# Three expert mixtures: every expert over all rows, or the chosen experts over gathered rows

## The reference

```python
# level 0, inside a block that has an attention z = x + attn(...) ahead of it
logits = h @ router_w                                   # h = layernorm(x)
expert_idx = jnp.argmax(logits, axis=-1)
for e in range(E):                                      # E = 4
    gv = h @ expert_wv[e]
    gate_raw, value = jnp.split(gv, 2, axis=-1)
    y = gate_raw * jax.nn.sigmoid(gate_raw) * value @ expert_proj[e]
    out = out + jnp.where((expert_idx == e)[..., None], y, 0.0)

# level 1
router_logits = jnp.einsum('bth,eh->bte', x, router_w)  # 8 experts
topk_values, topk_indices = jax.lax.top_k(router_logits, 2)
topk_weights = jax.nn.softmax(topk_values, axis=-1)
h1 = jax.nn.gelu(jnp.einsum('bth,efh->btef', x, w1) + b1, approximate=False)
expert_outputs = jnp.einsum('btef,ehf->bteh', h1, w2) + b2
topk_expert_outputs = jnp.take_along_axis(expert_outputs, topk_indices[..., None], axis=2)
mixed_output = jnp.sum(topk_expert_outputs * topk_weights[..., None], axis=2)

# level 2
scores = jax.nn.sigmoid(x_flat @ gate_w.T + gate_bias)
top_scores, top_idx = jax.lax.top_k(scores, 2)
top_scores = top_scores / (top_scores.sum(-1, keepdims=True) + 1e-06)
...                                                     # 8 gelu experts, as in level 1
shared = (jax.nn.gelu(x_flat @ sWu.T + sbu, approximate=False) @ sWd.T + sbd) * 0.1
return (combined + shared).reshape(b, s, h)
```

## Time and profile before

| | before |
|---|---|
| median of 3 runs | 2305.26 us (2302.99 to 2305.48) |
| span of the profiled execution | 2303.5 us |
| PE busy, matrix products | 1967.1 us (85%) |
| DVE busy | 1073.2 us (47%) |
| ACT busy | 821.1 us (36%) |
| POOL busy | 338.4 us (15%) |
| moved by the main DMA queue | 58.04 MB, 9.8% of 16 engines' span |

### The profile page before, as it was taken

How to read it: one execution, slowest core, us unless ns; L and a number is a source line. 1 busy time by engine, 2 the same in 40 slices (tenths; PEclk the granted TensorE clock), 3 DMA queues, 4 the chain that set the end, 5 groups by cost and what they waited for, 6 DMA issues and landing times. The chain is left out here.

```text
span 2303.5 us, 42189 instructions
## 1 busy us (share of the span) xinstructions
PE 1967.1 (85%) x17139; PEld 1357.5 (59%) x17156; DVE 1073.2 (47%) x2487; ACT 821.1 (36%) x1451; POOL 338.4 (15%) x572
## 2 busy tenths in 40 slices
PE   6869469799899986899997868999977786776998
PEld 4637136466676664677774546777755355454776
DVE  5456545433455555631117756211133845755432
ACT  1236124322222224644331046433333142134664
POOL 2242332100000003200000042000010511411000
PEclk9759589899999996999999969999987996988999
DMA  1052311000000015100000051000000000000000
GB/s 60 1 109 55 78 42 30 29 14 15 20 22 22 22 27 109 47 10 19 19 10 6 18 114 40 10 19 19 19 33 3 0 1 3 0 15 1 5 5 10
DMA packets 44754, 62.31 MB, mean 27 GB/s; under 512 B 4529, under 2 KB 38065, under 8 KB 44337
## 3 DMA queue, kind: packets, MB, share of 16 engines
q1 hardware_dynamic: 42834, 58.04, 9.8%
q10 hardware_dynamic: 1728, 1.57, 0.3%
HBM read 25.00 MB, written 1.05 MB: 11 GB/s over the span
## 5 line engine op out<-in xcount | busy, mean ns | idle before, releaser
L1913 ACT ACTIVATE l2f_a<-l2f_bank,l2f_expert 128x512 f32<-128x512 f32 x144 | 98.7, 687 | 137.6 <-PE l2f_bank L1849 137.6
L1860 PEld LDWEIGHTS l2f_bank<-l2f_expert,l2f_a 128*128 128x128 f32 x1152 | 134.1, 192 | 16.7 <-issue 16.7
L1860 PE MATMUL l2f_bank<-l2f_expert,l2f_a 128*128 128x128 f32 x1152 | 134.3, 275 | 0.0
L2038 DVE SCALAR_TENSOR_TENSOR X<-l2f_bank,l2f_W,X 128x128 f32<-128x128 f32 x144 | 40.5, 344 | 200.2 <-PE l2f_bank L1860 200.2
L1849 PE MATMUL l2f_bank<-l2f_xT,l2f_expert 128*128 128x512 f32 x288 | 132.2, 602 | 0.0
L1913 ACT ACTIVATE l1f_a<-l1f_bank,l1f_expert 128x512 f32<-128x512 f32 x128 | 87.8, 687 | 120.1 <-PE l1f_bank L1849 120.1
L1860 PEld LDWEIGHTS l1f_bank<-l1f_expert,l1f_a 128*128 128x128 f32 x1024 | 119.2, 192 | 14.8 <-issue 14.6
L2038 DVE SCALAR_TENSOR_TENSOR X<-l1f_bank,l1f_W,X 128x128 f32<-128x128 f32 x128 | 36.0, 344 | 181.0 <-PE l1f_bank L1860 180.9
L1860 PE MATMUL l1f_bank<-l1f_expert,l1f_a 128*128 128x128 f32 x1024 | 119.3, 275 | 0.0
L1849 PE MATMUL l1f_bank<-l1f_xT,l1f_expert 128*128 128x512 f32 x256 | 117.2, 601 | 0.0
L1467 DVE TENSOR_TENSOR l1a_kv<-l1a_bank,l1a_layer 128x512 f32<-128x512 f32 x96 | 61.8, 686 | 88.0 <-PE l1a_bank L1397 88.0
(11 more groups left out here) (605 smaller groups left out, 4158.4 us busy)
## 6 DMA issues: line engine op xcount, KB each, us to landing
l2f_expert<-in_experts_l2f SPq DMA_DIRECT2D x9, 514.0 KB, 3.7
l1a_layer<-in_layers_l1a SPq DMA_DIRECT2D x12, 385.0 KB, 3.0
l1f_expert<-in_experts_l1f SPq DMA_DIRECT2D x8, 514.0 KB, 3.7
l0x_k_stack<-l0x_k_parts SPq DMA_DIRECT2D x24, 128.0 KB, 3.2
l0g_k_stack<-l0g_k_parts SPq DMA_DIRECT2D x24, 128.0 KB, 2.5
l0f_expert<-in_experts_l0f SPq DMA_DIRECT2D x4, 768.0 KB, 4.3
l1x_k_stack<-l1x_k_parts SPq DMA_DIRECT2D x24, 128.0 KB, 3.0
l2x_k_stack<-l2x_k_parts SPq DMA_DIRECT2D x24, 128.0 KB, 3.5
```

The lines of the kernel that those rows point to most:

```text
L1860: ins = pe.matmul(self.banks[4 + par][:, i * D:(i + 1) * D], self.a[:, par, c, i * T:(i + 1) * T], w2[:, c, :], start=(c == 0), stop=(c == ...
L1913: act.activation(self.a[:, par, c, :], self.banks[c][:, :], ACT.Gelu, bias=self.buf[e % 2][:, 2 * FF + c:2 * FF + c + 1]).then_inc(q["gate ...
L2038: ins = dve.scalar_tensor_tensor(out=x, in0=self.banks[4 + u % 2][:, i * D:(i + 1) * D], scalar=self.W[:, g * GI + i, e:e + 1], in1=x, op0 ...
```

## The change

`Moe` computes for each row only the experts chosen for it. In place of the loop over units it has a loop over NT tiles of 128 rows that all belong to one expert; NT is the largest number that any routing can need: 19 in l0f, 39 in l1f and l2f, and all NT are always run.

Ranking: `choose` makes the one-hot mask, `count_rows` counts on PE the rows of each expert, `place_rows` turns counts and ranks into a position for each (row, choice), `mark` and `invert` build the inverse list by one-hot products (32 pairs of DVE instructions, 16 in l0f), and `find_rows` leaves `from_row` and `to_row`, one column of 128 indices per tile. Unused places get an index out of bounds, which the DMA skips.

Tile loop: SP stores the normalised rows to DRAM (`rows`). POOL gathers a tile's rows into one of ROWS_AHEAD = 4 buffers `xg`, PE turns it (`turn`), DVE copies it (`take_x`), then `up`, `activate`, in l0f `gate`, and `down` on 128 columns; DVE copies the result (`take_y`) to one of 4 buffers `y`, and POOL scatters it to DRAM (`results`). SP reads the number of the tile's expert from memory and loads it into one of EXPERTS_AHEAD = 4 buffers. After the last scatter SP reads `results` back in four pieces, and `combine` on DVE adds both choices to X with their weights. The bias stays a product with the turned W, now after the loop. l2f's shared expert stays dense (`wide_up`, `wide_activate`, `wide_down`, `wide_add`), placed around the ranking. The packed weights of the three stages take in the constant tables that the ranking needs (l0f 3 to 254 KB, l1f 68 to 392 KB).

```diff
+SORTED = {kind: (NB * T * TOP[kind] + ROUTES[kind] * (T - 1)) // T for kind in TOP}
+ROWS_AHEAD = 4
+EXPERTS_AHEAD = 4
...
+    def turn(self, pe, j):
+        q = self.q
+        pe.wait_ge(self.gathered[j % ROWS_AHEAD], self.moved(j))
+        if j >= 2:
+            pe.wait_ge(q["xt_ready"], j - 1)
+        pe.transpose(self.banks[6 + j % 2][:, 0:T], self.xg[j % ROWS_AHEAD][:, :], self.k.ident[:, :]).then_inc(q["turned"], 1)
...
+    def down(self, pe, j):
...
+        pe.wait_ge(q["gated"], j + 1)
+        if j >= 2:
+            pe.wait_ge(q["taken"], j - 1)
...
+        for c in range(FC):
+            ins = pe.matmul(self.banks[4 + j % 2][:, 0:D], self.a[:, j % 2, c, :], w2[:, c, :], start=(c == 0), stop=(c == FC - 1))
+        ins.then_inc(q["downed"], 1)
...
     def tensor(self, pe):
...
-        for u in range(1, self.steps):
-            self.up(pe, u)
-            self.down(pe, u - 1)
...
+        pe.wait_ge(self.q["to_ready"], 1)
+        self.turn(pe, 0)
+        self.turn(pe, 1)
+        for j in range(self.NT):
+            self.up(pe, j)
+            if j + 2 < self.NT:
+                self.turn(pe, j + 2)
+            if j:
+                self.down(pe, j - 1)
+        self.down(pe, self.NT - 1)
+        if not self.gated:
+            for g in range(NG):
+                self.turn_weights(pe, g)
+                self.bias(pe, g)
...
+    def mark(self, dve, c):
...
+        for m in range(c * CHUNK, (c + 1) * CHUNK):
+            dve.tensor_scalar(self.oneP[:, m, :], w["column"], self.split[:, 0, m:m + 1], None, ALU.is_equal)
+            ins = dve.scalar_tensor_tensor(out=self.oneJ[:, m, :, :], in0=w["starts"][:, 0:NT].unsqueeze(1).to_broadcast([P, 2, NT]),
+                                           scalar=self.split[:, 1, m:m + 1], in1=codes[:, m, :].unsqueeze(2).to_broadcast([P, 2, NT]),
+                                           op0=ALU.is_equal, op1=ALU.mult)
...
     def vector(self, dve):
...
+        for j in range(self.NT):
+            if self.gated:
+                self.gate(dve, j)
+            if j + 2 < self.NT:
+                self.take_x(dve, j + 2)
+            if j:
+                self.take_y(dve, j - 1)
...
+    def gather(self, pool, j):
+        rows = (self.from_row if self.K == 2 else self.to_row)[:, j:j + 1]
+        if j >= ROWS_AHEAD:
+            pool.wait_ge(self.q["turned"], j - ROWS_AHEAD + 1)
+        pool.indirect_dma_start(self.xg[j % ROWS_AHEAD][:, :], None, self.rows[:, :], bass.IndirectOffsetOnAxis(rows, 0),
+                                bounds_check=NB * T - 1, oob_is_err=False).then_inc(self.gathered[j % ROWS_AHEAD], 16)
+
+    def scatter(self, pool, j):
+        pool.wait_ge(self.q["taken"], j + 1)
+        pool.indirect_dma_start(self.results[:, :], bass.IndirectOffsetOnAxis(self.to_row[:, j:j + 1], 0), self.y[j % ROWS_AHEAD][:, :], None,
+                                bounds_check=self.M * T - 1, oob_is_err=False).then_inc(self.scattered[j % ROWS_AHEAD], 16)
+
+    def pool(self, pool):
...
+        for j in range(ROWS_AHEAD):
+            self.gather(pool, j)
+        for j in range(self.NT):
+            self.scatter(pool, j)
+            if j + ROWS_AHEAD < self.NT:
+                self.gather(pool, j + ROWS_AHEAD)
...
     def sync(self, sp):
...
-            sp.dma_start(self.buf[e % 2][:, :], self.stream[e, :, :]).then_inc(q[f"streamed{e % 2}"], 16)
...
+        for j in range(self.NT):
+            e = sp.value_load(self.expert_of[0:1, j:j + 1], min_val=0, max_val=self.NR - 1)
+            if j >= EXPERTS_AHEAD:
+                sp.wait_ge(q["downed"], j - EXPERTS_AHEAD + 1)
+            sp.dma_start(self.expert[j % EXPERTS_AHEAD][:, :], self.stream[bass.ds(e, 1), :, :].rearrange("e p c -> (e p) c"))\
+              .then_inc(self.streamed[j % EXPERTS_AHEAD], 16)
```

More of the change, by code:

```diff
@@ L1829, in bias @@
         ins.then_inc(q["bias_made"], 1)
[L1831 to L1862, removed]
     def tensor(self, pe):
+        chunks = self.M // CHUNK
         self.turn_rows(pe, 0)
@@ L1873, in tensor @@
         self.router(pe, 3)
-        for u in range(1, self.steps):
-            self.up(pe, u)
-            self.down(pe, u - 1)
[L1877 to L1881, removed]
+        if self.shared:
+            self.wide_up(pe, 0)
+            self.wide_up(pe, 1)
+        self.count_rows(pe)
+        if self.shared:
+            self.wide_down(pe, 0)
+            self.wide_up(pe, 2)
+            self.invert(pe, 0)
+            self.invert(pe, 1)
+            self.wide_down(pe, 1)
+            self.wide_up(pe, 3)
+            self.invert(pe, 2)
+            self.invert(pe, 3)
+            self.wide_down(pe, 2)
+            self.wide_down(pe, 3)
+        else:
+            for c in range(chunks):
+                self.invert(pe, c)
+        pe.wait_ge(self.q["to_ready"], 1)
[8 more added lines that the diff above has]
+        self.down(pe, self.NT - 1)
+        if not self.gated:
+            for g in range(NG):
+                self.turn_weights(pe, g)
+                self.bias(pe, g)
     def take_rows(self, act, g):
-        act.wait_ge(self.norms[g].turned, 1)
+        act.wait_ge(self.norms[g].turned, g + 1)
         xT = self.xT[:, g * GT:(g + 1) * GT]
@@ L1890, in take_rows, with wide_activate @@
         ins.then_inc(self.q["xT_ready"], 1)
-    def route_scalar(self, act):
+    def wide_activate(self, act, g):
         q = self.q
[L1894 to L1902, removed]
-        for c in range(FC):
[L1904 to L1914, removed]
+        for c in range(FC):
+            act.wait_ge(q["wide_up"], g * FC + c + 1)
+            if c == 0 and g >= 2:
+                act.wait_ge(q["wide_downed"], g - 1)
+            act.activation(self.wide[:, g % 2, c, :], self.banks[c][:, :], ACT.Gelu,
+                           bias=self.always[:, 2 * FF + c:2 * FF + c + 1]).then_inc(q["wide_gated"], 1)
@@ new lines, in activate @@
+    def activate(self, act, j):
+        q, buf = self.q, self.expert[j % EXPERTS_AHEAD]
+        if self.gated:
+            act.wait_ge(q["up"], (j + 1) * FC)
+            if j >= 2:
+                act.wait_ge(q["gated"], j - 1)
+            act.activation(self.sg[:, j % 2, :, :], self.banks[2 * (j % 2)][:, :].rearrange("p (c t) -> p c t", c=FC), ACT.Silu)\
+               .then_inc(q["silud"], 1)
+            return
+        for c in range(FC):
+            act.wait_ge(q["up"], j * FC + 2 * (c // 2) + 2)
+            if c == 0 and j >= 2:
+                act.wait_ge(q["downed"], j - 1)
+            ins = act.activation(self.a[:, j % 2, c, :], self.banks[2 * (j % 2) + c // 2][:, c * T:(c + 1) * T], ACT.Gelu,
+                                 bias=buf[:, 2 * FF + c:2 * FF + c + 1])
+        ins.then_inc(q["gated"], 1)
@@ new lines, in vector @@
+        for c in range(chunks):
+            self.mark(dve, c)
+            if self.shared and c == 1:
+                self.wide_add(dve, 0)
+        self.find_rows(dve)
+        if self.shared:
+            for g in range(1, NG):
+                self.wide_add(dve, g)
+        self.take_x(dve, 0)
+        self.take_x(dve, 1)
+        if not self.gated:
+            self.weigh(dve)
+        for j in range(self.NT):
+            if self.gated:
+                self.gate(dve, j)
[3 more added lines that the diff above has]
+                self.take_y(dve, j - 1)
```

495 lines of the change are left out of this document (371 added, 124 removed).

## The result

The changed kernel takes 2432.69 us (2425.14 to 2436.12, 4 runs) beside 2304.7 for the kernel before: a ratio of 1.0551, 95% interval 1.0532 to 1.057, slower by 128 us, where 133 were forecast and the range was 2250 to 2690. Its profiled execution spans 2423.3 us, at the low end of its runs.

What follows compares the result with a forecast made beforehand. The three mixture stages were taken as bound by PE's matrix work alone; the changed loops by one 6.9 us round per tile. Stage changes of -10.5, +83.0 and +60.7, sum +133.2, gave 2438 us; range 2250 to 2690.

Steps and rivals of the forecast that it cites:

- the round: Tile loops: down, take_y, scatter, gather, landing and turn pass once per tile, 6.9 us, 85 rounds beyond the first four tiles.
- DVE to POOL: In each round, the step from the end of take_y on DVE to POOL's scatter issue, 0.19 us.
- landing to turn: In each round, gathered rows land 1.5 us after the gather's issue, then 0.19 from DMA to PE.
- S and G: POOL's issue times in each round, S for the scatter and G for the gather, taken as 1.3 us each.
- the first up: Start of l1f's tile loop, after norms, ranking, mark, inversion and the first gather: 48 us after the stage begins.
- the tail: End of l1f and l2f after the loop: four bias rounds 15.0, then 32 additions and two waits 9.4, together 24.4 us.
- the first bias rounds: After the loop in l1f and l2f: four rounds of turn, copy and products, 3.75 us each with links.
- B: Rival, faster: POOL issues indirect DMAs as cheaply as SP plain ones, 0.39 each; kernel 2283, or about 2208; chance 0.21.
- C: Rival, faster: the buffers do look ahead, POOL's 2.6 us per tile or longer PE work repeats; some 2055 us; chance 0.04.
- D: Rival, slower still: the index column is walked dear, 2.69 us per issue at scatter and gather; kernel 2674; chance 0.13.

Runs made afterwards that it cites:

- the swap: Changed kernel with POOL issuing gather j+4 ahead of scatter j, nothing else changed; 2171.66 us, 0.9447 of the kernel before.
- e5_filler: Changed kernel in its own order, with 12 unread identity products put on PE between up j and the wait of turn j+2; 2368.54 us, ratio 1.0268.
- e6_first_eight: Changed kernel with gather ahead of scatter on POOL and ROWS_AHEAD 8 in place of 4; 2045.69 us, ratio 0.8881.

## Why the prediction was right, step by step

The step that carried it was read from the order of the lists, not from any duration: gather j+4 behind scatter j on POOL, turn j+4 ahead of down j+1 on PE. The waits view and the swap, which moves nothing else in the program, show it. The prices, in us, of the round at 1100.60:

| term | predicted | measured |
|---|---|---|
| down | 1.83 | 1.63 (1.06 at the full clock, in e5_filler) |
| PE to DVE, take_y | 0.04, 0.29 | 0.03, 0.29 |
| DVE to POOL | 0.19 | 0.80 |
| scatter issue | 1.3 | 1.01 |
| gap behind it | no term | 0.30 |
| gather issue | 1.3 | 1.02 |
| landing to turn | 1.5 + 0.19 | 1.65 |
| turn, until down begins | 0.27 | 0.17 |
| sum | 6.9 | 6.90 (mean of l1f 7.08) |

The sum is better than its terms. DVE to POOL was too small by 0.61: it was taken from a tensor operation, and an indirect DMA begins 0.61 later than that after its wait ends, 0.51 later than a plain DMA. The gap of 0.30 between two issues had no term. Scatter, gather, down and turn were too large by 0.29, 0.28, 0.20 and 0.10. The errors of 0.9 on either side cancel, which is luck; had only one side occurred, the forecast would have been off by some 77 us (0.9 x 85), still of the right sign. Pricing S and G by POOL's small tensors was a guess by the nearest rows that came out well, no knowledge of what an index costs.

The clock was taken as 0.50 from the earlier trace rows and is 0.67 in l1f's loop: PE works in bursts at both levels, and down lies between 1.06 and 1.92. e5_filler puts a price on what is lost by it, 0.75 of the round.

Stages: l0f 164.3 (forecast 176.4), l1f 327.1 (330.0), l2f 340.7 (336.5). In l1f the first up begins 47.7 us after the stage (forecast 48), the loop ends 258.6 later (257.6), and the tail takes 20.8 (24.4). Two terms there were too large: mark took 13.1 us, not 16.2, since a pair issues every 0.41 us and not every 0.51, and the first bias rounds ran at the higher clock, 2.35 each and not 3.75. That the first up still came on time is errors that cancel once more: from the end of mark to it, 7.1 us passed, not 5.1. l0f's forecast was 12 too high: behind its first up (3.24), the first tiles ran at the higher clock (up 1.95 for 16 instructions), where I had priced them at the lower.

Of the rivals, B fails on its condition (S + G below 1.03; together they are 2.03, with the gap 2.33). C had nearly the right time for another kernel: it said that only another order would allow some 2055, and with the gather first and eight buffers e6_first_eight is at 2046; the other order with four was at 2172. D fails on the price of the indices: an issue with 128 of them takes 1.01 us, a plain one 0.54. On this the Trainium skill ("GPSIMD Engine Reference", section "Performance pitfalls for Q7 kernels") has about 102 cycles for each small read, which would have been 10.9 us per issue, the prediction's estimate; the trace's 1.01 us doesn't bear that out for this DMA. The Trainium skill's other page ("DMA: Bandwidth & Descriptors", section "Anatomy of one DMA — SWDGE (gpsimd) path") is nearer with 2.0 us and the bytes, an estimate of 2.15 to landing, where the trace has 2.6. It calls the generation of descriptors small; the trace has no row for that alone, but the whole issue occupies POOL for 1.01 us.

What stays open: why a plain DMA lands 0.9 us later after its issue than an indirect one (the places that the latter skips are 17% of the bytes), and what POOL does in the 0.5 us by which an indirect DMA starts later after a wait. A doubled gather (two tiles by one issue) and a PE list with turn behind down were not tried.

## What to carry to other kernels

Count buffers by the order of the lists, not by their number: four buffers looked ahead by nothing, because the refill of a buffer stood behind the result of the tile that the consumer was about to make. Ask of each refill which unfinished work stands ahead of it on its own engine, and of each consumer what it stands ahead of; the distance in tiles between the two is the look-ahead, and the round divided by it is about the period, until an engine's own work is longer. And work removed from PE can cost the clock of the work that is left, if the time won is only waited away.

## What the runs showed of the hardware

An indirect DMA of 128 rows of 512 bytes occupies POOL for 1.01 us, with 0.30 between two and 0.80 between the end of the releasing DVE instruction and its start; a plain one for 0.54, without a gap and with 0.29. The rows of the indirect gather, at most 64 KB, land 2.6 us after the issue begins, the 64 KB of the plain one 3.1 (l1f). In e6_first_eight, with the DMA engines at a share of 0.79 and 248 GB/s, the gather's landing rose to 4.4 and the expert's from 3.5 to 4.8.

The same loop had a granted clock of 0.67 with PE busy for 51% (76.55 of 150 us) and of 0.99 with the added products (113.62 us, 76%), while a later stage of the kernel before had 0.50 with 71%. The share alone doesn't tell the clock.
